# A DLRM tower: last group's flat layer transposed, its norm carried as a factor, 8 of 32 sample columns merged late

## The reference

```python
x = layer_norm(dense @ Wd.T, gd, bd)                      # (512, 128)
y = layer_norm(einsum('bnd,ed->bne', e, Ws), gs, bs)       # (512, 26, 128)
y = layer_norm(einsum('bne,pn->bep', y, Wsi), gsi, bsi)    # over p: 32
T = concatenate([x[:, None, :], swapaxes(y, 1, 2)], 1)     # (512, 33, 128)
Z = einsum('bnd,bmd->bnm', T, T)
Zflat = Z[:, TRIL_I, TRIL_J]                               # 528 entries
z = layer_norm(Zflat @ Wl.T, gl, bl) * mask                # 512 wide, 384 kept
h = relu(concatenate([z, dense], 1) @ W_top1 + b_top1)     # 512
h = relu(h @ W_top2 + b_top2)                              # 256
out = h @ W_top3                                           # (512, 1)
```

## Time and profile before

| | us |
|---|---|
| median of 3 runs | 181.03 (178.66 to 181.64) |
| the profiled execution | 180.52 |
| its span | 178.7 |
| PE busy | 149.9 (84%) |
| DVE busy | 119.9 (67%) |
| POOL busy | 107.4 (60%) |
| ACT busy | 79.3 (44%) |

### The profile page before, as it was taken

The page is one execution under the profiler, slowest core; times in us unless marked ns, Lnnn a source line. Parts: engine busy times, 40 slices in busy tenths (PEclk is TensorE's granted clock), DMA queues, the critical chain, the costliest instruction groups (busy, mean ns, idle before and its releaser), DMA issues.

```text
span 178.7 us, 3313 instructions
## 1 busy us (share of the span) xinstructions
PE 149.9 (84%) x1189; PEld 103.1 (58%) x1189; DVE 119.9 (67%) x326; ACT 79.3 (44%) x221; POOL 107.4 (60%) x138
## 2 busy tenths in 40 slices
PE   0365494898889999599998979999999999789894
PEld 0163353364656676285566749656978664485682
DVE  0703776791888467879687699885689799857300
ACT  3104112233786455454255555623647644751251
POOL 5777777777777777777777777777772004620000
PEclk9999758589999999879999999999999999999999
DMA  5511299111111112331111233111122200000000
GB/s 173 180 23 28 51 366 349 33 27 30 29 24 33 22 29 47 74 77 26 33 24 29 48 76 71 28 27 29 24 40 66 51 12 0 2 4 0 0 0 0
DMA packets 9729, 9.76 MB, mean 55 GB/s; under 512 B 3665, under 2 KB 7377, under 8 KB 9458
## 3 DMA queue, kind: packets, MB, share of 16 engines
q0 software_dynamic: 3328, 3.41, 10.1%
q1 hardware_dynamic: 5954, 5.18, 9.3%
q10 hardware_dynamic: 432, 0.97, 1.6%
HBM read 7.98 MB, written 0.00 MB: 45 GB/s over the span
## 4 chain that ended last, share of the span: by engine, by line
PE 59%; DVE 16%; POOL 10%; issue 6%; ACT 5%; DMA 3%; ACTq 0%; POOLq 0%
POOL emb L388 10%; PE pz L483 10%; PE pc L447 8%; PE py L468 6%; PE pf L499 6%; PE tu L430 5%; PE pf L518 3%; PE tu L420 3%; DVE y_ms L1087 3%; DMA emb<-tables_dram,rows_at 2%; PE py L463 2%; PE pf L545 2%; PE py L499 2%; PE pf L525 2%; DVE T L1096 2%
## 5 line engine op out<-in xcount | busy, mean ns | idle before, releaser
L388 POOL DMA_INDIRECT emb<-tables_dram,rows_at x104 | 99.8, 960 | 32.9 <-issue 29.9
L447 PE MATMUL pc<-wbd,emb 128*128 128x192 f32 (+4 forms) x128 | 29.0, 336 | 1.1 <-DVE emb L1081 1.1
L447 PEld LDWEIGHTS pc<-wbd,emb 128*128 128x128 f32 x128 | 20.4, 202 | 16.5 <-issue 13.7
L483 PE MATMUL pz<-T 128*64 128x67 f32 x512 | 22.6, 231 | 5.9 <-DVE T L1096 4.8
L483 PEld LDWEIGHTS pz<-T 128*64 128x64 f32 x512 | 18.1, 139 | 14.1 <-issue 6.7
L755 ACT ACTIVATE embT<-tu 128x256 f32<-128x256 f32 x26 | 9.8, 379 | 33.0 <-PE tu L420 33.0
L1087 DVE TENSOR_REDUCE y_ms<-ysq 128x16 f32<-128x512 f32 x32 | 20.4, 679 | 5.6 <-ACT ysq L770 5.5
L420 PE MATMUL tu<-proj_w,emb 128*128 128x128 f32 x52 | 12.5, 306 | 10.4 <-DMA emb<-tables_dram,rows_at 10.4
L1096 DVE TENSOR_TENSOR T<-py,y_r 128x512 f32<-128x512 f32 x32 | 20.6, 687 | 0.6
L770 ACT ACTIVATE ysq<-py 128x512 f32<-128x512 f32 x32 | 17.3, 593 | 6.7 <-PE py L468 6.6
L430 PE MATMUL tu<-mbd,embT 128*128 128x128 f32 x104 | 17.8, 297 | 0.5 <-ACT embT L755 0.5
(11 more groups left out here) (142 smaller groups left out, 201.5 us busy)
## 6 DMA issues: line engine op xcount, KB each, us to landing
emb<-tables_dram,rows_at POOLq DMA_INDIRECT x104, 2.5
z<-gram SPq DMA_DIRECT2D x48, 32.0 KB
w<-w_dram SPq DMA_DIRECT2D x1, 1280.0 KB
wl<-wl_dram SPq DMA_DIRECT2D x1, 1024.0 KB
denseT<-denseT_dram ACTq DMA_DIRECT2D x1, 512.0 KB, 5.1
w<-w_dram SPq DMA_DIRECT2D x1, 512.0 KB
comb_w<-comb_w_dram ACTq DMA_DIRECT2D x1, 311.0 KB, 3.1
sel<-sel_dram SPq DMA_DIRECT2D x1, 240.0 KB, 4.7
```

Of the source, the lines that this page charges most:

```text
L388: pool.indirect_dma_start(emb[:, 2 * pair + half, :], None, t["tables"], bass.IndirectOffsetOnAxis(ap=rows_at[:, 2 * g + half, j:j + 1], a ...
L447: mm = pe.matmul(PC[m % NPC][:, :, :].rearrange("p b c -> p (b c)")[:, col:col + n], of, wbd[:, :, :].rearrange("p b c -> p (b c)")[:, at: ...
L483: mm = pe.matmul(PZ[2 * PR * h:2 * PR * h + 2 * PR, ITEMS * b:ITEMS * (b + 1)], of[:, 0:2 * PR], of, start=True, stop=True)
```

## The change

Preparation, new:
- At tick 35 `bias_rows` on PE: 12 products of w1 (128x128 weights) with one column of bl, into `PF`; at tick 38 DVE adds b1 (`bias_of_bl`). `dense_layer` takes all 512 samples, with this sum as the copy's bias.
- At tick 41 ACT scales the three kept blocks of w1 by gl (`scale_w1`). `z_scaled` is a plain copy then.
- `scale_wl` and `wl5_copy` also sum each row (`accum_out`), DVE makes -1/512 of the sums (ticks 40 and 48), and ACT adds these means (`centre_wl` at ticks 46, 50, 54, 58; `centre_wl5` at 52), so that the flat layer's output has mean zero over its 512 columns.
- A thirteenth load, `b2_row` (1 KB), before w3.

Group 2: its linear features are copied by POOL after the gathers and no longer by DVE; `flat_layer(2, 4)` waits for POOL.

Last group:
- POOL stacks columns 0 to 15 (after four gram copies of the group), then 16 to 23 (after six). DVE merges these 24 (`early_merge`), and only then does its part of the late stacking, of columns 24 to 31, and merges those (`late_merge`). The linear features are shared by ACT (two) and POOL (two).
- The flat layer has `wl` as weights and `zm` as moving data: four chunks of 128 outputs, five products of 128 columns each. DVE copies each chunk to `f_raw`, ACT squares it, PE sums the squares over all partitions with a matrix of ones, and ACT takes the root: `sd`, the same in all partitions.
- f_raw isn't divided by sd. The rest of the first layer (`dense_sd`) and b2 are multiplied by sd, relu passes the factor through, and DVE multiplies the last row by 1/sd. `mlp1_dense`, `mlp1_rest`, the statistics and the transposes of this group are gone.

```diff
+CHUNKS = [3, 0, 1, 2]
...
-EARLY = NB // 2
+EARLY = [slice(0, NB // 2), slice(NB // 2, NB - NB // 4)]
+LATE = slice(NB - NB // 4, NB)
+LATE_LOADS = 13
...
-            pool.wait_ge(gram_ready, NG * QUARTERS - QUARTERS // 2)
             pool.wait_ge(f_done, last - 1)
+            pool.wait_ge(gram_ready, last * QUARTERS)
+            for pair in range(STEPS - 6, STEPS):
+                pool.wait_ge(gathered[pair], 32)
             for a in range(4):
-                for r in range(4):
-                    pool.tensor_copy(z[last % 2][PR * r:PR * r + PR, :, a, :, 0:EARLY], folded(last, a, r, slice(0, EARLY)))
+                of = gram[PR * a:PR * a + PR, (last - 1) % 2, :, :]
+                pool.tensor_copy(zx[(last - 1) % 2][0:PR, a, :], of[:, 2 * PR + a % 2, :])
+                i = pool.tensor_copy(zx[(last - 1) % 2][ROW_S:ROW_S + PR, a, :], of[:, ITEMS - 1, :])
+            i.then_inc(zx_pool_ready, 1)
+            for samples in EARLY:
+                pool.wait_ge(gram_ready, last * QUARTERS + samples.stop // SLOTS)
+                for a in range(4):
+                    for r in range(4):
+                        i = pool.tensor_copy(z[last % 2][PR * r:PR * r + PR, :, a, :, samples], folded(last, a, r, samples))
+                i.then_inc(early_stacked, 1)
             pool.wait_ge(gram_ready, NG * QUARTERS)
             for a, r in POOL_PARTS:
-                i = pool.tensor_copy(z[last % 2][PR * r:PR * r + PR, :, a, :, EARLY:], folded(last, a, r, slice(EARLY, NB)))
+                i = pool.tensor_copy(z[last % 2][PR * r:PR * r + PR, :, a, :, LATE], folded(last, a, r, LATE))
             i.then_inc(late_stacked, 1)
+            for a in (2, 3):
+                of = gram[PR * a:PR * a + PR, last % 2, :, :]
+                pool.tensor_copy(zx[last % 2][0:PR, a, :], of[:, 2 * PR + a % 2, :])
+                i = pool.tensor_copy(zx[last % 2][ROW_S:ROW_S + PR, a, :], of[:, ITEMS - 1, :])
+            i.then_inc(zx_late_ready, 1)
...
+            def last_flat_layer(n):
+                o = CHUNKS[n]
+                if n == 0:
+                    pe.wait_ge(merged, NG + 1)
+                wait_if_any(pe, f_raw_ready, n - 1)
+                for k in range(KC):
+                    pe.matmul(last_flat(o), wl[:, k, P * o:P * o + P], zm[(NG - 1) % 2][:, k, :, :].rearrange("p a b -> p (a b)"),
+                              start=(k == 0), stop=False)
+                if n == 0:
+                    pe.wait_ge(zx_xs_ready, NG)
+                    pe.wait_ge(zx_late_ready, 2)
+                pe.matmul(last_flat(o), wl5[0:ROWS_X, P * o:P * o + P], zx[(NG - 1) % 2][0:ROWS_X, :, :].rearrange("p a b -> p (a b)"),
+                          start=False, stop=True).then_inc(flat_done, 1)
+            def square_sums(n):
+                o = CHUNKS[n]
+                pe.wait_ge(f_sq_ready, n + 1)
+                pe.wait_ge(f_raw_ready, OUT // P - 1)
+                mm = pe.matmul(variance, ones[:, :], f_sq[:, o, :], start=(n == 0), stop=(n == OUT // P - 1), skip_group_check=True)
+                if n == OUT // P - 1:
+                    mm.then_inc(var_done, 1)
+            def bias_rows():
+                pe.wait_ge(l_late, 16 * LATE_LOADS)
+                pe.wait_ge(wl5_ready, 1)
+                for m in range(H1 // P):
+                    for c in range(KEPT // P):
+                        mm = pe.matmul(PF[:, m:m + 1], w1[:, c, P * m:P * m + P], glbl[:, 1, c:c + 1],
+                                       start=(c == 0), stop=(c == KEPT // P - 1))
+                mm.then_inc(bl_done, 1)
             def dense_layer(m):
                 if m == 0:
-                    pe.wait_ge(l_late, 16 * 12)
-                    pe.wait_ge(wl5_ready, 1)
+                    pe.wait_ge(b1_ready, 1)
                 wait_if_any(pe, d1_ready, m)
                 for c in range(DENSE // P):
-                    mm = pe.matmul(PF[:, 0:(NG - 1) * GROUP], w1[:, 3 + c, P * m:P * m + P], denseT[:, c, 0:(NG - 1) * GROUP],
...
+                    mm = pe.matmul(PF[:, :], w1[:, 3 + c, P * m:P * m + P], denseT[:, c, :],
...
+            def last_mlp1(c):
+                pe.wait_ge(f_raw_ready, CHUNKS.index(c) + 1)
+                for m in range(H1 // P):
+                    pe.matmul(layer1(NG - 1, m), w1[:, c, P * m:P * m + P], f_raw[:, c, :], start=(c == 0), stop=False)
+            def last_dense(m):
+                pe.wait_ge(dense_sd_ready, m // 2 + 1)
+                pe.matmul(layer1(NG - 1, m), ident, dense_sd[:, m, :], start=False, stop=True).then_inc(m1_done, 1)
+            def last_bias2():
+                pe.wait_ge(sd_ready, 1)
+                pe.wait_ge(y_ready, NG - 1)
+                for m in range(H2 // P):
+                    pe.matmul(layer2(NG - 1, m), b2_row[0:1, P * m:P * m + P], sd[0:1, :], start=True, stop=False)
...
+                if tick == 35:
+                    bias_rows()
...
-            mlp1_dense(last, 1)
             gram_products(end, 0)
+            mlp1(last - 1, 0)
             gram_products(end, 1)
-            mlp1(last - 1, 0)
-            mlp1_dense(last, 2)
             mlp1(last - 1, 1)
-            mlp1_dense(last, 3)
             mlp1(last - 1, 2)
             mlp1(last - 1, 3)
-            flat_layer(last, 0)
-            flat_layer(last, 1)
-            flat_layer(last, 2)
-            flat_layer(last, 3)
-            flat_layer(last, 4)
+            last_flat_layer(0)
+            last_flat_layer(1)
+            last_flat_layer(2)
+            last_flat_layer(3)
+            square_sums(0)
+            square_sums(1)
+            square_sums(2)
+            last_mlp1(0)
+            square_sums(3)
             mlp2(last - 1)
-            z_transposes(last)
+            last_mlp1(1)
             mlp3(last - 1)
-            mlp1_dense(last, 0)
-            mlp1_rest(last, 0)
-            mlp1_rest(last, 1)
-            mlp1_rest(last, 2)
-            mlp1_rest(last, 3)
+            last_mlp1(2)
+            last_dense(0)
+            last_dense(1)
+            last_dense(2)
+            last_dense(3)
+            last_bias2()
             mlp2(last)
             mlp3(last)
...
+            def scale_w1(c):
+                act.wait_ge(bl_done, 1)
+                act.activation(w1[:, c, :], w1[:, c, :], ACT.Copy, scale=glbl[:, 0, c:c + 1]).then_inc(w1_ready, 1)
+            def last_squares(n):
+                act.wait_ge(f_raw_ready, n + 1)
+                act.activation(f_sq[:, CHUNKS[n], :], f_raw[:, CHUNKS[n], :], ACT.Square, scale=float(OUT) ** -0.5).then_inc(f_sq_ready, 1)
+            def last_sd():
+                act.wait_ge(var_done, 1)
+                act.activation(sd[:, :], variance, ACT.Sqrt, bias=eps[:, :]).then_inc(sd_ready, 1)
+            def late_linear(g):
+                for a in range(2):
+                    of = gram[PR * a:PR * a + PR, g % 2, :, :]
+                    act.activation(zx[g % 2][0:PR, a, :], of[:, 2 * PR + a % 2, :], ACT.Copy)
+                    i = act.activation(zx[g % 2][ROW_S:ROW_S + PR, a, :], of[:, ITEMS - 1, :], ACT.Copy)
+                i.then_inc(zx_late_ready, 1)
...
-                act.activation(wl[:, k, :], wl[:, k, :], ACT.Copy, scale=gg[:, 0, k:k + 1]).then_inc(wl_ready, 1)
+                act.activation(wl[:, k, :], wl[:, k, :], ACT.Copy, scale=gg[:, 0, k:k + 1], accum_out=wl_sum[:, k:k + 1]).then_inc(wl_summed, 1)
+            def centre_wl(k):
+                act.wait_ge(wl_m_ready, 1)
+                act.activation(wl[:, k, :], wl[:, k, :], ACT.Identity, bias=wl_m[:, k:k + 1]).then_inc(wl_ready, 1)
...
+                for k in pairs_at(tick, 46, KC):
+                    centre_wl(k)
+                if tick == 52:
+                    centre_wl5()
                 for g in groups_at(tick, -38, NG - 1):
                     x_sums_copy(g)
                 if tick == 1:
                     x_scaled()
                 if tick == 23:
                     wl5_copy()
+                if tick == 41:
+                    for c in range(KEPT // P):
+                        scale_w1(c)
...
-            late_stack(last, slice(EARLY, NB))
+            late_stack(last, LATE)
+            late_linear(last)
             h1_relu(last - 1)
-            f_spread(last)
+            last_squares(0)
+            last_squares(1)
+            last_squares(2)
+            last_squares(3)
+            last_sd()
             h2_relu(last - 1)
-            z_scaled(last)
             y_copy(last - 1)
             h1_relu(last)
             h2_relu(last)
-            y_copy(last)
...
+            def turn_and_choose(g, samples, n):
+                dve.stream_shuffle(zm[g % 2][:, ::-1, :, samples].rearrange("p k a b -> p a k b"), z[g % 2][:, 1, :, :, samples],
+                                   [PR - 1 - i for i in range(PR)]).then_inc(turned, 1)
+                dve.wait_ge(turned, n)
+                dve.copy_predicated(zm[g % 2][:, :, :, samples],
```

(31 more changed lines are left out.)

139 lines of the change are left out of this document (92 added, 47 removed).

## The result

The changed kernel takes 186.81 us (median of five runs, 184.21 to 189.38), the kernel before 180.23 us on the same chip (178.66 to 181.64): ratio **1.0328, 95% interval 1.0197 to 1.0459**. The ratio compares the means of the fast runs on either side (185.86 and 179.96 us), while the traced execution of the changed kernel, at 188.89 us, is one of its two slow runs. The forecast was 186.5 us, with 0.78 on slower by over 2%. That is where it came out, though the interval reaches just under 2%. The profiled execution took 188.89 us (span 187.0, mean granted clock 0.927); that of before took 180.52 us (span 178.7, clock 0.952). This trace shows 8.4 us more, and the medians 6.6; part of the difference between the two is TensorE's clock, to which the experiments come.

What follows compares the result with a forecast made beforehand. The prediction took TensorE, busy 84% of the span, to bound the kernel. It added 4.9 us for preparation, 0.9 for the last merge and 0.15 from the flat layer on, 5.95 on 180.52, giving 186.5 us, range 182.0 to 190.0.

Steps and rivals of the forecast that it cites:

- The preparation: Making the weights ready, 45 to 70 us: added work on PE and ACT delays the chain by 4.9 us.
- (a): `bias_rows` on PE at tick 35: 24 weight loads take 2.6 us, 1.4 us left over after PE's idle 1.19.
- (b): `dense_layer` on PE streams 512 columns instead of 384: 16 instructions add 1.7 us, all on the chain.
- (c): ACT's added scaling, centring and wider dense copies: 6.3 us of work, with PE waiting 1.1 us for a gram copy.
- Everything behind is in the same order, so the delay should travel whole: After the preparation: the delay reaches the end undiminished, as the gathers can't take it back.
- 130 to 158 us: Group 2's linear copies go from DVE to POOL and `mlp1_dense` leaves PE: counted 0, at best 1.4 us gained.
- The last merge: Last gram copy to flat layer: POOL's second 16 copies hold up DVE's early merge, flat layer 0.9 us later.
- From the flat layer on: Flat layer to end of the y copy: 15.2 us in total against 15.02 before, +0.15 us.
- The clock falls in the tail: Rival: PE's granted clock falls after its wait before the flat layer, costing 1.7 us; 188.2 us, chance 0.20.
- The reverse at 76 us: Rival: the clock fall at 76 us doesn't come; 184.8 us, chance 0.06.
- The preparation hides: Rival: slack at 70 to 74 us absorbs most of the preparation; +2.75, 183.3 us, chance 0.20.
- The faster ending: Rival: last merge and norm end sooner and the preparation lies in the shade of waits; 177.2 us, chance 0.04.

Runs made afterwards that it cites:

- e4: The changed kernel unaltered, run again for a second trace; ratio 1.0334 to the kernel before.
- e1: The kernel before with only the new preparation and 512-column dense layer, old last group kept; ratio 1.0291 to the kernel before.
- e12: The kernel before with `bias_rows` alone at tick 35, result unused, each product streaming 128 columns instead of one; ratio 1.0165 to the kernel before.
- e2: The changed kernel without `bias_rows`, `bias_of_bl`, `scale_w1`, the centring and its sums, 512-column dense layer kept; ratio 1.0257 to the kernel before.
- e5: The changed kernel without `bias_rows` and `bias_of_bl`; ratio 1.0139 to the kernel before.
- e7: The changed kernel with `bias_rows` streaming 128 columns of the dense input instead of one column of bl; ratio 1.0303 to the kernel before.
- e11: The kernel before with one-column `bias_rows` alone at tick 35, its result unused; ratio 1.0237 to the kernel before.
- e10: The kernel before with only the changed kernel's last merge, 24 columns early and 8 late; ratio 1.0066 to the kernel before.
- e3: The changed kernel with DVE's late stacking put ahead of the early merge; ratio 1.0347 to the kernel before.
- e6: The changed kernel without `scale_w1`, the means and the centring, `bias_rows` and the wide dense layer kept; ratio 1.0385 to the kernel before.
- e8: The changed kernel with `bias_rows`, dense layer, centring and `scale_w1` moved to ticks 66 to 101; ratio 1.082 to the kernel before.
- e9: The kernel before with DVE merging columns 0 to 15 early and 16 to 31 after the late copies; ratio 0.9965 to the kernel before.

## Why the prediction came out right, point by point

The direction, and the size of the preparation and of the merge, were forecast from their causes. That the total came within 0.3 us of the median is in part luck. Both traces of the changed kernel show more than the 5.95 us of the sum between their ends: 8.30 us here and 9.23 in e4, and over the eleven timed executions the median is 188.3 us and not 186.8. What the sum mainly left out is TensorE's clock: the fall behind `bias_rows`, which is in every profile that has it, and falls at 76 to 80 us or in the tail, which come in some executions and not in others.

**The preparation, +4.9 us; measured +5.44 (5.68 to 5.70 in e1 and e4).** The sum is near, its parts aren't all.
- (a) `bias_rows`, 2.6 us and 1.4 behind the idle 1.19: 2.66 and, in e12, 1.43. The Trainium skill, "TensorE: Matmul & The Clock Gate", "LDWEIGHTS (loading the stationary operand)", gives 107 ns for such a load; the trace agrees (0.11 us from start to start), and the 25 ns between starts of "Wait — 56ns, not 53.3ns?" is not what bound here.
- (b) dense stream, +1.7: e2 shows +1.83.
- (c) the ACT block, +1.8 beyond (a) and (b): e5 less e2 gives **0.85**. This is the term that was mis-sized. The block ran from 57.37 to 59.3 (forecast 56.0 to 58.2), but PE had a dense block and a combine step to do meanwhile: the gram product that I had waiting 1.1 us for the copy starts at 59.97 without a wait, and of the later dense blocks one waits, 0.45 us. In e5, without `bias_rows`, PE waits for that copy for 0.26 us; in e7, with it, not at all. So the sign "PE waiting for an ACT gram copy right behind the `scale_w1` block" was not seen in the changed kernel. The accumulator reads lay beside the next instruction, as taken. Timeline of ACT, changed kernel, where the next one starts 0.09 us after the read:

```profile
48.70 0.19 ACT L932 ACTIVATION_READ_ACCUMULATOR wl<-wl,gg 128x1 f32 x1
48.79 0.31 ACT L861 ACTIVATE y_sd<-y_ms,eps 128x32 f32<-128x32 f32 x1
```

- Not in the sum: the clock behind `bias_rows`, **1.50 us** (e11 less e12), 1.57 in the changed kernel (e4 less e7). The prediction had a fall of the clock as a rival, but in the tail, behind a wait.
- These four make 1.43 + 1.83 + 0.85 + 1.5 = 5.6. The over-sized queue (0.95 too much) covered the larger part of a fall that wasn't thought of (1.5), and that is luck.

**"Everything behind is in the same order, so the delay should travel whole": right but for the clock.** Without a fall the stretch from the eighth to the last copy grows by 0.05 us (e4 against e10). The 0.90 of the profile is a fall that cost 1.70 us in the changed kernel and 0.85 in the one before.

**130 to 158 us, 0 ("at best 1.4 gained"): measured +0.23** from the 27th copy to the last (13.98 us against 13.75). It is a sum of three terms of which the prediction had one: 0.47 gained by DVE's relief, 0.49 lost to the wait for the stacking DMA, and 0.22 lost by the order ahead of the last gram product.

**The last merge, +0.9: measured +0.73, and +0.86 alone (e10).** Step by step as forecast: POOL 4.32 us for the 16 half-size copies (4.3), DVE's early merge behind POOL, seven copies 1.48 us (1.4).

**From the flat layer on, +0.15: measured +0.75.** `mlp2(last)` starts 12.27 us after the flat layer; 104 instructions at 0.112 had given 11.65. The mis-sized part is the pitch: in seven places where one group of products gives way to the next, 0.08 to 0.10 us are added, two of them in `last_bias2`, which takes 0.63 us (181.32 to 181.95) and not 0.45. The sd root was ready 6.93 us after the start, 6.9 forecast, and held nothing up.

**The rivals.** The clock falls in the tail, given 0.20: in this kernel's two traces once, at 1.43 us against the 1.7 given (and in e3, e6 and e7, which have the same work in the last group, but not in e5 and e8). Its 188.2 us is what six of the eleven executions took (188.3 to 189.8), so it would have deserved about even odds beside my own case. The reverse at 76 us came in e4, and is worth 1.70 there, as forecast; between before and e10 the fall at that place is worth 0.85. "The preparation hides" (183.3) fails by (b) alone, and by e1. The faster ending fails by e10.

## What to carry to other kernels

Before PE work goes into a free place of a tuned order, price it by the number of weight loads, and look at what it does to the granted clock behind it: a stream of one column between loads cost 1.5 us more than the same loads with 128 columns. Price a term from the same stretch in several traces before its whole-kernel ratio: e2, with less work than e5, took longer. Work that comes late only because a helper needs long for its share (here POOL, 4.3 us for a quarter of the columns) is better split where the helper is done anyway, as e9 did with its 16 columns: 0.37 us sooner in its trace, though not told from noise in its time. Moving a chain through four static queues into somebody's idle time costs more than the work itself, unless each link is checked for what stands behind it (e8).
